# Moving the transposed half of a Gram product to the end of TensorE's step, making bias rows on the chip, and splitting the first load

## The reference

```python
q = _conv1x1(Wq, bq, y).reshape(B, H, Dh, -1)
k = _conv1x1(Wk, bk, y).reshape(B, H, Dh, -1)
v = _conv1x1(Wv, bv, x).reshape(B, H, Dh, Lx)
scores = jnp.einsum('bhdl,bhel->bhde', q, k) / jnp.sqrt(jnp.float32(E))
attn = jax.nn.softmax(scores, axis=-1)
out = jnp.einsum('bhde,bhel->bhdl', attn, v).reshape(B, E, Lx)
o = _conv1x1(Wo, bo, out) + x
mu = jnp.mean(o, axis=(1, 2), keepdims=True)
var = jnp.var(o, axis=(1, 2), keepdims=True)
o_hat = (o - mu) * jax.lax.rsqrt(var + EPS)
return o_hat * gn_w[None, :, None] + gn_b[None, :, None]
```

## Time and profile before

| | us |
|---|---|
| median of 3 runs | 187.91 |
| lowest and highest | 186.92 and 188.99 |
| the profiled execution | 188.77 |
| its span, first to last instruction | 187.0 |
| busy in the span: PE, PEld, DVE, ACT, POOL | 172.1, 127.9, 150.4, 140.3, 114.1 |

### The profile page before, as it was taken

The page is one execution under the profiler, slowest core; times in us unless marked ns, Lnnn a source line. Parts: engine busy times, 40 slices in busy tenths (PEclk is TensorE's granted clock), DMA queues, the critical chain, the costliest instruction groups (busy, mean ns, idle before and its releaser), DMA issues. The chain is left out here.

```text
span 187.0 us, 4165 instructions
## 1 busy us (share of the span) xinstructions
PE 172.1 (92%) x996; PEld 127.9 (68%) x996; DVE 150.4 (80%) x554; ACT 140.3 (75%) x354; POOL 114.1 (61%) x170
## 2 busy tenths in 40 slices
PE   7777999999999999999999999999999999998640
PEld 7666776767777777777776777877777777765310
DVE  1746888999998998989989999899889999975531
ACT  4425588888888888888888988888888988777032
POOL 3775577766766677767776677667676777611020
PEclk9979999999999999999999999999999999999785
DMA  6798769898988889989888987988889755522223
GB/s 210 262 417 329 254 197 306 316 288 311 330 294 302 314 282 337 341 294 324 315 301 289 319 333 300 332 297 276 324 315 317 254 209 213 204 117 112 112 112 112
DMA packets 14409, 50.83 MB, mean 272 GB/s; under 512 B 1728, under 2 KB 1856, under 8 KB 14400
## 3 DMA queue, kind: packets, MB, share of 16 engines
q1 hardware_dynamic: 13968, 50.34, 75.7%
q10 hardware_dynamic: 432, 0.40, 0.8%
HBM read 33.95 MB, written 16.78 MB: 271 GB/s over the span
## 5 line engine op out<-in xcount | busy, mean ns | idle before, releaser
L506 PE MATMUL o_ps<-x_sb,m_sb 128*128 128x512 f32 x128 | 71.5, 647 | 0.0
L506 PE MATMUL g_ps<-hl_sb 128*128 128x258 f32 x256 | 47.0, 308 | 0.6 <-DVE hl_sb L416 0.6
L416 DVE TENSOR_TENSOR hl_sb<-y_sb,hl_sb 128x512 fp32r<-128x512 f32 x64 | 44.3, 693 | 2.4 <-ACT hl_sb L325 2.4
L269 POOL TENSOR_TENSOR rstd<-veps,nhalf 128x1 f32<-128x1 f32 x32 | 27.3, 853 | 26.9 <-DVE veps L421 26.9
L297 POOL TENSOR_TENSOR lsuma<-hl_sb 128x256 f32<-128x256 f32 x32 | 23.8, 743 | 30.2 <-DVE hl_sb L416 30.2
L325 ACT CAST hl_sb<-y_sb 128x512 fp32r<-128x512 f32 x64 | 39.1, 614 | 4.0 <-DMA y_sb<-in_ctx_dram 4.0
L362 ACT ACTIVATE out_sb<-o_ps,shift,gain 128x1024 f32<-128x1024 f32 (+1 forms) x32 | 38.3, 1198 | 0.2
L506 PEld LDWEIGHTS g_ps<-hl_sb 128*128 128x128 f32 x256 | 35.6, 195 | 0.8 <-issue 0.8
L506 PEld LDWEIGHTS ps_ps<-wqT,g_sb 128*128 128x128 f32 x64 | 9.7, 191 | 24.9 <-DVE g_sb L444 19.0
L452 DVE BATCH_NORM_STATS2 bn<-o_ps 128x6 f32<-128x512 f32 x32 | 22.3, 698 | 4.9 <-PE o_ps L506 1.2
L284 POOL TENSOR_TENSOR lsum<-lsuma,lsumb 128x256 f32<-128x256 f32 x32 | 23.3, 727 | 4.3
(11 more groups left out here) (57 smaller groups left out, 309.8 us busy)
## 6 DMA issues: line engine op xcount, KB each, us to landing
y_sb<-in_ctx_dram SPq DMA_DIRECT2D x32, 512.0 KB, 4.8
x_sb<-in_x_dram SPq DMA_DIRECT2D x32, 512.0 KB, 5.0
out_dram<-out_sb SPq DMA_DIRECT2D x31, 512.0 KB, 4.2
out_dram<-out_sb SPq DMA_DIRECT2D x2, 256.0 KB, 2.2
w_in<-in_weights_dram ACTq DMA_DIRECT2D x1, 256.0 KB, 8.8
rows<-in_biases_dram ACTq DMA_DIRECT2D x1, 128.0 KB, 6.5
cols<-in_columns_dram ACTq DMA_DIRECT2D x1, 3.0 KB, 3.4
```

What stands on the lines that cost most here:

```text
L269: nc.gpsimd.tensor_tensor(rstd[:, h1:h1 + 1], veps[:, h1:h1 + 1], nhalf[:, :], ALU.pow).then_inc(rstd_ready, 1)
L416: nc.vector.tensor_tensor(hl_sb[:, ky, chunks, C:2 * C], y_sb[:, ky, chunks, :], hl_sb[:, ky, chunks, 0:C].bitcast(F32), ALU.subtract).the ...
L506: return nc.tensor.matmul(dst, lhsT, rhs, start=start, stop=stop, **more)
```

## The change

On TensorE the transposed block and the sum of l of a batch move from the next step (between the two big products) to the end of the same step, behind the scores. The eight Gram products stay together, in two halves with a wait for each half of l, ahead of the products of `m_ps`. The last batch's softmax product no longer stands ahead of the second big product. VectorE copies `g_sb` and `s_sb` ahead of `zinv` and of both `bn_stats`, and makes `p_sb` ahead of `bn_aggr`. For the first batch, GpSimd's sum of l is replaced by eight TensorE products of l with `ones_r` (`EARLY`).

The broadcast load `rows` is gone. VectorE makes two diagonal matrices from `ident` and the columns bq and bk, one TensorE product of 256 columns makes `bqB` and `bkB` of them in PSUM, and ScalarE copies both. `k0` is made in VectorE's step 2, `wqT` ahead of it; the constants from `cols` are made ahead of VectorE's step 0, behind a wait for that load. The first y tile is loaded in two DMAs of 256 KB, one per half of its positions, and ScalarE's first rounding waits for the first of them. `WARM_UP` is 8 for 12.

```diff
-GRAM_BEFORE_M = 6
-WARM_UP = 12
+EARLY = 1
+WARM_UP = 8
 FILL = 2
...
         @block.sync
-            for k in range(UNROLL):
+            part = HALF
+            sp.dma_start(y_slot(0)[:, 0:part], batch_y(0)[:, 0:part]).then_inc(y_first, 16)
+            sp.dma_start(y_slot(0)[:, part:L], batch_y(0)[:, part:L]).then_inc(y_in[0], 16)
+            for k in range(1, UNROLL):
                 sp.dma_start(y_slot(k), batch_y(k)).then_inc(y_in[k], 16)
...
         @block.gpsimd
-                if has(t, 1):
+                if has(t, 1) and not is_step(t, EARLY):
...
         @block.scalar
             act.dma_start(cols[:, :], columns).then_inc(c_loaded, 16)
-            act.dma_start(rows[:, :, :].rearrange("p v e -> p (v e)"),
-                          biases.rearrange("(a v) e -> a (v e)", a=1).broadcast_to([P, 2 * E])).then_inc(c_loaded, 16)
             act.dma_start(w_in[:, :, :].rearrange("p w c -> p (w c)"), weights).then_inc(w_loaded, 16)
...
                 if ahead:
+                    if is_step(t, 0):
+                        act.wait_ge(y_in[k], 16)
                     round_half(1)
+                if is_step(t, 0):
+                    act.wait_ge(rows_ready, 1)
+                    nc.scalar.copy(bqB[:, :], row_ps[:, 0, :]).then_inc(rows_copied, 1)
+                    nc.scalar.copy(bkB[:, :], row_ps[:, 1, :]).then_inc(rows_copied, 1)
...
         @block.vector
+            dve.wait_ge(c_loaded, 16)
+            nc.vector.tensor_scalar(diag[:, 0, :], ident[:, 0:P], bq_raw, SCALE * E, ALU.mult, ALU.mult).then_inc(const_dve, 1)
+            nc.vector.tensor_scalar(diag[:, 1, :], ident[:, 0:P], bk_raw, -float(E), ALU.mult, ALU.mult).then_inc(const_dve, 1)
+            nc.vector.tensor_scalar(bq_col[:, :], bq_raw, -SCALE * L, None, ALU.mult).then_inc(const_dve, 1)
+            nc.vector.tensor_copy(ident[:, P:P + 1], bo).then_inc(const_dve, 1)
...
                 if has(t, 1):
                     rest_half(-1, 1)
+                if has(t, 2):
+                    dve.wait_ge(g_ready, t - 1)
+                    nc.vector.tensor_tensor(g_sb[:, :], g_ps[:, 0:C], b2_sb[:, :].bitcast(F32), ALU.add).then_inc(g_copied, 1)
+                    nc.vector.tensor_copy(s_sb[:, :], s_ps).then_inc(s_copied, 1)
                 if is_step(t, 2):
-                    dve.wait_ge(w_loaded, 16)
-                    nc.vector.tensor_scalar(wqT[:, :], w_in[:, 0, :], -SCALE, None, ALU.mult).then_inc(const_dve, 1)
+                    dve.wait_ge(rows_copied, 2)
+                    nc.vector.scalar_tensor_tensor(out=k0[:, :], in0=bkB[:, :], scalar=bq_col[:, :],
...
-                if has(t, 2):
-                    dve.wait_ge(g_ready, t - 1)
-                    nc.vector.tensor_tensor(g_sb[:, :], g_ps[:, 0:C], b2_sb[:, :].bitcast(F32), ALU.add).then_inc(g_copied, 1)
-                    nc.vector.tensor_copy(s_sb[:, :], s_ps).then_inc(s_copied, 1)
...
             step(0, 1)
-            dve.wait_ge(c_loaded, 16 * N_CONST)
-            nc.vector.tensor_scalar(bqB[:, :], rows[:, 0, :], -SCALE, None, ALU.mult).then_inc(const_dve, 1)
...
+            dve.wait_ge(w_loaded, 16)
+            nc.vector.tensor_scalar(wqT[:, :], w_in[:, 0, :], -SCALE, None, ALU.mult).then_inc(const_dve, 1)
             pipeline(dve, step, begin=2)
...
         @block.tensor
-            pe.wait_ge(const_dve, 4)
+            pe.wait_ge(const_dve, 6)
+            product(row_ps[:, :, :].rearrange("p v e -> p (v e)"), onesn[:, :],
+                    diag[:, :, :].rearrange("p v e -> p (v e)")).then_inc(rows_ready, 1)
+            keep_busy(FILL)
...
+                if has(t, 4):
+                    products_of_x(1)
+                if has(t, 2):
+                    query_product()
+                if has(t, 3):
+                    softmax_product()
                 if has(t, 1):
+                    pe.wait_ge(l_ready, t * 2 - 1)
+                    if exists(t, 2):
+                        pe.wait_ge(s_copied, t - 1)
+                    gram_products(range(0, HCH))
                     pe.wait_ge(l_ready, t * 2)
-                    if exists(t, 2):
-                        pe.wait_ge(s_copied, t - 1)
-                    gram_products(range(0, GRAM_BEFORE_M))
+                    last = gram_products(range(HCH, CH))
+                    if is_step(t, EARLY):
+                        for c in range(CH):
+                            last = product(g_ps[:, 2 * C:HL], hl_sb[:, 0, c, C:2 * C], ones_r[:, :], start=False,
+                                           skip_group_check=True)
+                    last.then_inc(hl_ready, 1)
...
-                if has(t, 1):
-                    gram_products(range(GRAM_BEFORE_M, CH)).then_inc(hl_ready, 1)
...
                     product(sc_ps, wqT[:, :], sbk_sb[:, :], start=False).then_inc(sc_ready, 1)
+                if has(t, 1):
+                    pe.wait_ge(b2_copied, t)
+                    transposed = product(g_ps[:, 0:C], b2_sb[:, :], ident_r[:, :], start=False, skip_group_check=True)
+                    if is_step(t, EARLY):
+                        transposed.then_inc(g_ready, 1)
+                    else:
+                        pe.wait_ge(lsum_ready, t - EARLY)
+                        product(g_ps[:, 2 * C:HL], lsum[:, h1, :], ones_r[:, :], start=False,
+                                skip_group_check=True).then_inc(g_ready, 1)
+                if is_step(t, 1) or is_step(t, 2):
+                    keep_busy(FILL)
```

More of the change, by code:

```diff
@@ L421, in variance @@
                     nc.vector.tensor_scalar(veps[:, h1:h1 + 1], var_ps, -1.0, EPS, ALU.mult, ALU.add).then_inc(veps_ready, 1)
-                if has(t, 5) and not is_step(t, RUSH + 1):
+                if has(t, 5):
                     variance()
@@ L458, in step @@
                                             ALU.add).then_inc(mrow_ready, 1)
-                if has(t, 2):
-                    dve.wait_ge(s_copied, t - 1)
-                    dve.wait_ge(p_ready, t - 1)
-                    nc.vector.scalar_tensor_tensor(out=p_sb[:, :], in0=bqB[:, :], scalar=s_sb[:, :],
-                                                   in1=p_ps, op0=ALU.mult, op1=ALU.add).then_inc(p_copied, 1)
                 if has(t, 0):
@@ L557, in mean, with gram_products @@
                     product(mu_ps, onesn[:, :], mrow[:, h:h + 1]).then_inc(mu_ready, 1)
+                def gram_products(chunks):
+                    kg = (k - 1) % UNROLL
+                    for c in chunks:
+                        mm = product(g_ps[:, 0:HL], hl_sb[:, kg, c, 0:C], hl_sb[:, kg, c, :],
+                                     start=(c == 0), stop=(c == CH - 1))
+                    return mm
                 if has(t, 5) and not is_step(t, RUSH + 1):
@@ L570, in step @@
                     variance()
-                if has(t, 2):
-                    pe.wait_ge(b2_copied, t - 1)
-                    product(g_ps[:, 0:C], b2_sb[:, :], ident_r[:, :], start=False, skip_group_check=True)
-                    if is_step(t, 2):
-                        keep_busy(FILL)
-                    pe.wait_ge(lsum_ready, t - 1)
-                    product(g_ps[:, 2 * C:HL], lsum[:, h, :], ones_r[:, :], start=False,
-                            skip_group_check=True).then_inc(g_ready, 1)
-                if is_step(t, 2):
-                    keep_busy(FILL)
-                if has(t, 3) and is_step(t, RUSH):
-                    softmax_product()
                 if has(t, 4):
@@ L587, in step @@
                     query_product()
[L588 removed]
+                if has(t, 3):
                     softmax_product()
[L591 to L597 removed]
                 if has(t, 1):
[L600 removed]
+                    pe.wait_ge(l_ready, t * 2 - 1)
                     if exists(t, 2):
                         pe.wait_ge(s_copied, t - 1)
[L604 removed]
+                    gram_products(range(0, HCH))
+                    pe.wait_ge(l_ready, t * 2)
+                    last = gram_products(range(HCH, CH))
[4 more added lines that the diff above has]
+                    last.then_inc(hl_ready, 1)
                 if has(t, 3):
```

76 lines of the change are left out of this document (37 added, 39 removed).

## The result

| | before | changed |
|---|---|---|
| median (lowest to highest), us | 187.41 (186.5 to 188.99) | 176.33 (176.13 to 176.6) |
| profiled execution, span | 188.77, 187.0 | 176.6, 174.8 |

A forecast was written before the change was run, and what follows sets the result against it. TensorE looked fully busy, but its 0.21 us stall per step waiting for `g_sb` left room. Start 2.7, full steps 5.8 and end 0.8 sum to 9.3 us, taking 187.91 to 178.6 us; 8-in-10 range 175.0 to 184.5.

The forecast's parts named there:

- The stall behind the second big product: Full steps: TensorE's query product waits for `g_sb`, 0.21 us a step, plus up to 0.1 for starting again.
- The rival in which only start and end gain: Full steps stay at 5.05 us because something else takes up the stall's gain; 184.4 us in all, chance 0.15.
- the one in which the start gains nothing: Start: weights and tile 1 as late as ever, a loss of 0.7 us; 182.0 us in all, chance 0.13.
- the slower one, a wait for `b2_sb`: End of each TensorE step: this wait replaces the one for `g_sb`; 195.4 us if 0.8 late, chance 0.07.
- the fourth, in which the parts cancel: Half the stall comes back elsewhere and the start loses 0.7 us; about 186 us in all, chance 0.05.
- three start-to-start loops: Full steps: TensorE 4.72 to 4.82 us, VectorE 4.80, ScalarE 4.63; step taken as 4.85, gaining 5.8 us.
- VectorE's loop: Full steps: big products through second `bn_stats` and `m_sb` to the next big product, 4.80 us, the longest loop.
- (b): Start: without the broadcast load its DMA hole goes, weights land some 3 us earlier, tile 1 rounded from about 6.3.
- (d): Start: first half of tile 0 comes 0.8 us earlier at most; costed at nothing, as tile 1 covers it.
- Step (c): Start: from tile 1 at 6.3, the first query product comes at 9.3, 2.3 us earlier.
- (a): Start: eight early TensorE products replace GpSimd's sum for batch 0, 0.14 us each or 1.1 us; free.
- The clock's bonus: End: shorter idle may keep TensorE's clock up for two big products, up to 1.7 us, not in the sum.

The follow-up runs named there:

- g_behind_stats: Changed kernel with `g_sb` and `s_sb` back behind VectorE's first `bn_stats`, TensorE's order staying new: 188.18 us, ratio 1.012 to the kernel before.
- block_between: Changed kernel with the transposed block and sum product back between TensorE's two big products, VectorE's order staying new: 183.55 us, ratio 0.989 to the kernel before.
- short_stats: Changed kernel whose second `bn_stats` reads 384 of its 512 columns, so outputs differ from the reference: 175.93 us, ratio 0.947 to the kernel before.
- seven_products: Changed kernel without the last of each batch's eight Gram products, so outputs differ from the reference: 175.08 us, ratio 0.943 to the kernel before.
- unsplit_unrolled: unsplit with all steps of all engines written out, no hardware loops: 174.21 us, ratio 0.925 to the kernel before.
- unsplit: Changed kernel with the first y tile loaded in one DMA again: 175.78 us, ratio 0.942 to the kernel before.
- rows_load: Changed kernel with the old broadcast load of bq and bk back between `cols` and the weights, its data unused: 179.17 us, ratio 0.960 to the kernel before.

## Why the prediction was right, and where its steps were off

**The mechanism.** The stall behind the second big product was the thing to look for, its chain ran over `bn_stats` and `g_sb`, and the two moves together took it away. g_behind_stats and block_between show that neither does alone. The rival in which only start and end gain fell with a pace of 4.80; the one in which the start gains nothing, with 2.44 us; the slower one, a wait for `b2_sb`, with `b2_sb` ready 0.26 us early. The time of the fourth, in which the parts cancel, was added up wrong: with half of 5.8 and the end's 0.8 gained and 0.7 lost it is 184.9, not 186.

**The full steps: 7.26 us for 5.8.** The term mis-sized is the pace, 4.80 for 4.85. I added three start-to-start loops and took the longest, VectorE's 4.80, plus 0.05 for disturbance. VectorE's loop wasn't 4.80. Its piece of 2.79 us, from the second `bn_stats` to the next big product, got shorter by the place of `p_sb`, of which I had said that it changes the order in this chain and not its length. The kernel before, timeline of VectorE behind the second `bn_stats` at 102.14:

```profile
102.94 0.21 DVE L455 BATCH_NORM_AGGREGATE mv<-bn 128x2 f32<-128x12 f32 x1
...
103.32 0.34 DVE L463 SCALAR_TENSOR_TENSOR p_sb<-bqB,s_sb,ps_ps 128x128 f32<-128x128 f32 x1
103.57 0.69 DVE L416 TENSOR_TENSOR hl_sb<-y_sb,hl_sb 128x512 fp32r<-128x512 f32 x1
```

There `bn_aggr` started 0.80 us behind the start of the statistics, 0.10 after their end, and the rounding rest (`hl_sb`) 1.43 behind. In the changed kernel `p_sb` fills the gap, starting 0.62 behind, and the rest starts 1.24 behind (100.22 to 101.46): 0.19 us less. The piece still shows 2.73, since `dev` comes late: the rest takes 0.80 us here for 0.69, and in short_stats, where VectorE is 0.13 us earlier, `dev` starts no sooner and waits for TensorE's mean. Less the 0.19, my sum is 4.61, and seven_products, with steps of 4.65 to 4.70, bounds the loop from above. No run has the old place of `p_sb` alone, so what that move gives is not measured; by the sum, some 0.07 us of each step would be lost without it, an estimate from 4.80 and 4.73. TensorE's own work, 5.03 less the stall and less the slow restart, was 4.72 by my sum and is 4.73. The other 0.07 of the mean is the hardware loop's turn: in the tight order four steps with a turn take 19.2 us rather than 18.9, and unsplit_unrolled, at 4.74, has none of it. I had put 0.02 on the turn. Already the kernel before had steps of 5.01 and 5.02 with one of 5.17 at each turn, 0.04 on the mean; the tight order made it 0.07.

**The start: 2.44 us for 2.7, by two errors that cancel.** (b) held in its first half: the broadcast made the hole, and without it the weights land by 6.0. (d) failed. I costed the split of the first load at nothing, since tile 1 would cover what it gives. I did not ask what it takes from tile 1: 1.2 to 1.3 us of the whole kernel. Step (c) had tile 1 rounded from 6.3, and it was 7.65; the query product came 0.8 later than forecast. (Without the split the two were 5.89 and 8.87 in unsplit, 6.45 and 9.88 in unsplit_unrolled.) From there to step 4 it went faster than I had it: 6.37 us for 7.33, 0.96 gained for 0.4. That is the granted clock, 1.00 for 0.57, and not the new order: rows_load and g_behind_stats have the new order of these steps, their clock fell to 0.50 there, and they took 7.34 us each, as the kernel before. It is in part luck. In the eight traces that start as the changed kernel does, or nearly so, the clock held in six and fell in two, g_behind_stats and seven_products (7.10 us). (a) is free here, as costed, with 0.95 us for the eight products (0.12 each for my 0.14), and it is worth 1.5 us in unsplit.

**The end: 2.5 us for 0.8.** The order gave 0.75 in step 34, as forecast. The clock's bonus, which I named with up to 1.7 and left out of the sum, came nearly whole, 1.5. That is the largest single miss. The bonus comes in most executions and not in all, so it should have carried a chance and its share of the sum.

**How much is the clock.** By the two traces 0.96 + 1.5 = 2.5 of the 12.2 us are a clock that held where it had fallen. The runs of the kernel before with the highest mean clock, 0.99, took 185.2 to 185.7 us, and the changed kernel 176.1 to 177.6 in its eight runs. So some 9 us are the change's own, an estimate. That this is near the forecast's 9.3 owes something to misses that cancel: the full steps gave 1.5 more than forecast, the query product 0.8 less.

**What I said the profile would show.** The waits for `g_sb` did not vanish (5.7 us left), since a weight load may wait under a running product; the distance of 1.80 us was the better sign. Query product, pace, first big product of step 4 (16.45 for 16.2), weights and step 34's second big product (start 1.80 before the softmax product at 161.96, no gap) came as said; so did the filled DMA engines at 5 to 7 us.

**Left open.** Why the halved load moves less at a full DMA share; how the broadcast stops the other queue; what exactly the loop's turn waits for; what decides whether the clock falls at the start and the end, from which the scatter of the kernel before (185.2 to 190.5) seems to come, since its runs get longer as their mean clock goes from 0.99 to 0.945; and what fewer warm-up products (`WARM_UP`) did, which no run separates.

## What to carry to other kernels

Judge a full engine by the distance between starts, not by its busy row, and remember that a loop summed from such distances holds gaps that a new order can fill: here an instruction moved into the gap behind the statistics shortened the chain by 0.19 us. Look at the granted clock of a stretch before crediting its gain to a new order. Where two engines run fixed orders, a producer moved earlier pays only together with its consumer, so cost the half-done change too. At the start, look at what each load does to the landing of the next one: a half load or a broadcast can cost more there than it brings.

## What the hardware showed that was not expected

A 512 KB load cut into two of 256 KB, 2 KB for each partition, moved 260 to 277 GB/s from 3 to 6 us where the whole moved 364 to 432, at a DMA share of 0.79 to 1.13 and 1.00 to 1.09 (240 to 367 with the second tile cut). A 128 KB broadcast load left a hole of 57 to 79 GB/s in a full stretch and held the load behind it back by 3 us. The turn of a hardware loop cost some 0.3 us in a coupled order on four engines. And one and the same order of instructions met either level of the clock: at the start the way from the query product to step 4 took 6.2 to 6.4 us at a granted clock of 1.00 and 7.1 to 7.3 where it fell to 0.50, and at the end from step 33 on 18.7 to 19.3 us or 20.3.
